# Two edits near the end of an attention stage: idle transposes confined to the last slot, and the last element's expert shares computed between its pick and its ranks

## What is computed

```
x = layernorm(x + attn(x, x, causal=True),  ln1)
x = layernorm(x + attn(x, ctx, causal=False), ln2)      # 16 heads of width 16
w = softmax(x @ router_w + router_b)                    # 8 experts
topw, topi = top_k(w, 2);  topw = softmax(topw)         # the two shares of a row
out = sum over e of combine[t, e] * (gelu(x @ w1[e] + b1[e]) @ w2[e] + b2[e])
x = layernorm(x + out, ln3)
```

## Time and profile before

| | us |
|---|---|
| median of 3 runs | 1198.77 |
| lowest, highest | 1197.58, 1203.42 |
| the profiled execution, its own time | 1199.14 |
| its span from first to last instruction | 1197.4 |
| attention block ends (barrier), on the span's clock | 880.5 |
| expert block | 880.5 to 1197.4 |

### The profile page before, as it was taken

One profiled execution on the slowest core, in us unless ns is written; L12 is line 12 of the kernel. 1 busy time (PEld: TensorE's weight loads), 2 busy tenths in 40 slices (PEclk: granted clock), 3 DMA queues, 4 the chain that ended last, 5 costly groups with the idle time before them and its releaser, 6 DMA issues. The chain is left out here.

```text
span 1197.4 us, 27891 instructions
## 1 busy us (share of the span) xinstructions
PE 1078.9 (90%) x9323; PEld 899.4 (75%) x9323; DVE 845.6 (71%) x2539; ACT 759.7 (63%) x1587; POOL 519.6 (43%) x736
## 2 busy tenths in 40 slices
PE   8688989999999999998899989888989999999960
PEld 7356666768888888876667666655779999999960
DVE  2777888777766666657777677664368888888856
ACT  4355565667666666655566666545258898888842
POOL 4355555322122213445667346442333454444554
PEclk9699999999999999999999999998989999999995
DMA  7685756654344433445656556531646877877774
GB/s 168 99 182 80 90 82 115 91 95 65 52 63 63 72 54 54 77 55 77 85 129 116 114 116 108 91 71 58 228 151 181 250 252 229 239 229 234 232 198 145
DMA packets 110893, 152.41 MB, mean 127 GB/s; under 512 B 23104, under 2 KB 95296, under 8 KB 104384
## 3 DMA queue, kind: packets, MB, share of 16 engines
q1 hardware_dynamic: 100560, 138.64, 52.2%
q0 software_dynamic: 8352, 10.80, 4.6%
q10 hardware_dynamic: 1872, 1.60, 1.1%
HBM read 78.39 MB, written 21.62 MB: 84 GB/s over the span
## 5 line engine op out<-in xcount | busy, mean ns | idle before, releaser
L996 ACT ACTIVATE probs<-s 128x384 f32<-128x384 f32 (+1 forms) x512 | 263.7, 541 | 127.2 <-PE s L771 113.8
L1080 DVE TENSOR_REDUCE neg_max<-s 128x2 f32<-128x512 f32 x256 | 168.1, 688 | 72.7 <-PE s L743 66.0
L771 PE MATMUL s<-q_stack,k_stack 98*128 98x256 bf16 (+1 forms) x1024 | 175.0, 261 | 10.6 <-ACT probs L996 8.1
L626 POOL TENSOR_SCALAR_AFFINE_SELECT probs<-probs 128x256 f32<-128x256 f32 x256 | 104.0, 418 | 173.4 <-ACT probs L996 171.0
L1077 DVE CUSTOM_DVE_ANT_0 s<-s,mask_qk 128x256 f32<-128x256 f32 x256 | 114.2, 446 | 64.4 <-PE s L740 56.6
L771 PEld LDWEIGHTS s<-q_stack,k_stack 98*128 98x128 bf16 x1024 | 87.2, 98 | 40.9 <-ACT probs L996 28.6
L793 PE MATMUL pv<-probs,v 128*32 128x256 f32 (+1 forms) x2048 | 111.1, 357 | 4.7 <-POOL probs L626 4.7
L743 PE MATMUL s<-k_stack,q_stack 96*128 96x256 bf16 x512 | 95.6, 275 | 14.4 <-DVE neg_max L1080 11.9
L1467 PE MATMUL moe<-rows_hi,e_w_hi 128*128 128x256 f32 x368 | 103.6, 282 | 2.0 <-DVE rows_lo L1585 2.0
L1467 PE MATMUL moe<-e_w_hi,e_hidden_hi 128*128 128x256 f32 x368 | 104.6, 284 | 0.0
L1467 PE MATMUL moe<-rows_hi,e_w_lo 128*128 128x256 f32 x368 | 103.0, 280 | 0.0
(11 more groups left out here) (209 smaller groups left out, 2913.1 us busy)
## 6 DMA issues: line engine op xcount, KB each, us to landing
w<-in_expert_w SPq DMA_DIRECT2D x26, 1024.0 KB, 5.4
k_stack<-k_part SPq DMA_DIRECT2D x192, 128.0 KB, 4.0
q_stack<-q_part SPq DMA_DIRECT2D x180, 128.0 KB
w_next<-in_expert_w SPq DMA_DIRECT2D x22, 1024.0 KB, 5.3
rows<-slots_x SPq DMA_DIRECT2D x25, 256.0 KB
slots_x<-filler SPq DMA_DIRECT2D x8, 518.0 KB
cT<-in_context SPq DMA_DIRECT2D x16, 256.0 KB, 5.7
e_b<-in_expert_b SPq DMA_DIRECT2D x24, 128.0 KB
```

Of the source, the lines that this page charges most:

```text
L626: pool.affine_select(out=blocks, in_=blocks, compare_op=ALU.is_ge, fill=0.0, base=0, pattern=[[0, TILES], [1, P]], channel_multiplier=-1). ...
L771: last = pe.matmul(dst[:, kt * S:kt * S + S - q0], k[:, kt * P:(kt + 1) * P], q[:, q0:S], start=True, stop=True)
L996: act.activation(probs_of(n, hd)[:, 0:width], s2[hd % 2][:, 0:width], ACT.Exp, scale=SCALE).then_inc(probs_ready, 1)
L1080: dve.tensor_reduce(neg_max[:, :, hd], src[:].rearrange("p (t s) -> p t s", t=TILES), AX_X, ALU.max, negate=True).then_inc(s1_free, 1)
```

## The change

The condition of the 12 transposes goes from n >= 27 to n == 31, and that of the 10 from lanes 2 to 6 to lane 6 alone. The `share` steps of lane 7 get times of their own, ahead of `rank` and `place`.

```diff
-DRAIN = NCALL - 5
+LAST_SHARES = (67.0, 68.0, 68.3, 70.0)
@@ plan_call
-        steps += [(at + later, "share", lane, i) for i, at in enumerate(AT["shares"])]
+        steps += [(at + later, "share", lane, i) for i, at in enumerate(LAST_SHARES if lane == B - 1 else AT["shares"])]
@@ scores
-                if n >= DRAIN and hd == H - 2:
+                if n == NCALL - 1 and hd == H - 2:
                     pe.wait_ge(u_ready, weighed_so_far[0])
                     idle(WARM_EXPS)
@@ final_T
-                if 2 <= lane < B - 1:
+                if lane == B - 2:
                     idle(WARM_NORM, dst)
```

## The result

The changed kernel took 1202.68 us (median of 20 runs, 1199.41 to 1207.4), the kernel before 1198.45 us (20 runs, 1195.96 to 1203.42). The ratio is 1.0033, 95% interval 1.0024 to 1.0041, so 2.9 to 4.9 us slower, centre 4.0. The forecast was 2 us faster (1196.8, range 1193.0 to 1202.0). The sign was wrong, and the median lies 0.7 us over the range; the change is still within the 0.5% in which I had put 0.91.

What follows compares the result with a forecast made beforehand. It took PE as busy 90% of the span, with unread transposes on the path in slots 27 and 28 only. Terms -3.5 + 0 + 2.4 - 0.9 = -2.0 took 1199.1 to 1197.1, with runs' median 0.4 lower: 1196.8, range 1193.0 to 1202.0.

Steps and rivals of the forecast that it cites:

- Slots 27 and 28: First parts of both slots shorten by 1.75 us each without the batches: -3.5 us, bounds 0 and -4.9.
- rival (D): Second parts of slots 27 and 28 shrink too: -4.9 + 2.4 - 0.9 = -3.4 us, 1195.4; chance 0.08.
- Rival (C): Second parts of slots 27 and 28 swallow their first parts' gain: +1.5 us, 1200.3; chance 0.15.
- Slots 29 and 30 start nothing earlier: PE waits for ACT and POOL behind the batches there, so removal gives 0 us at an unchanged clock.
- That they fall, and where: PE's clock falls once each in slots 29 and 30, near 794 to 799 and 821 to 826 us.
- Rival (A): The clock holds through slots 29 and 30: -3.5 - 0.9 = -4.4 us, 1194.4; chance 0.12.
- What a fall costs: Slower clock in slots 29 and 30: 1.2 us a slot, +2.4 us in all, bounds 0 and +6.8.
- the short spell: The 3.40 us stretch at 1.2 GHz near 851 in the earlier trace, taken as each fall's length in slots 29 and 30.
- Rival (B): Falls in slots 29 and 30 last 6.81 us and reach PE-bound work: +2.4 us in all, 1201.2; chance 0.22.
- The shares: Lane 7's last share comes 0.9 us earlier and all of it reaches the barrier: -0.9 us, bounds -0.9 and +0.3.
- The sum: Whole kernel: -3.5 + 0 + 2.4 - 0.9 = -2.0 us, forecast 1196.8; chance 0.43.

Runs made afterwards that it cites:

- `cut_27_28_shares`: Kernel before without the 12 and 10 unread transposes in slots 27 and 28 alone, plus lane 7's shares moved ahead: ratio 0.9974, repeated 0.9977.
- `cut_27_28_fill`: `cut_27_28_shares` plus 22 unread transposes in slot 29, 8 before head 7's maxima product and 14 before head 11's: 0.9942 of the kernel before, repeated 0.9959.

## Why the prediction was wrong

**Slots 27 and 28: right.** Forecast -3.5 us; the traces give 55.5 to 52.0, so -3.5, and timing gives -2.9 (-5.2 to -0.6). But that the two agree to the tenth is luck. The first parts shrank by 1.38 and 1.39 us, not 1.75, since POOL pauses 0.49 us ahead of the inverse root (L566) in slots 27 and 28 and not in slot 26, whether the batches are there or not. The rest is slot 28's second part (19.20 to 17.92 in the first pair), which the sum left alone and I had as bound and rival (D). It isn't bound to the edit either: slot 28 takes 28.3 to 28.4 us in four traces with the batches and 27.1 in three, among them both further traces of the kernel before. What the edit surely takes out is the 1.4 us a slot. Rival (C), the gain swallowed, is out.

**Slots 29 and 30 start nothing earlier: right.** POOL is waited for instead, 1.24 and 1.40 us, and the final transposes start 6.44 and 6.11 us behind L750 (6.36 and 6.06 before).

**That they fall, and where: right.** Forecast 794 to 799 and 821 to 826 us on the old clock; 794.4 and 825.1, that is 796.2 and 826.0 when counted from each slot's L750. Rival (A) is out.

**What a fall costs: this is the step that failed.** I took from the earlier trace rows "the short spell", 3.4 us, for each of the two slots, and 0.7 of half of it. Of the two factors one held. The price per microsecond at 1.2 GHz was about right: forecast 2.4 us for 6.8, 0.35 each; measured 6.6 us by timing (5.9 by the table) for 23.9 - 4.9 = 19.0 us more of it, 0.35 (0.31), and 0.26 by the plain medians. The length was wrong by a factor of near 3: the two spells last 6.8 to 10.2 us each in the four traces without either batch, and a shorter one follows at about 812 us, as it did before. Rival (B) named this mechanism and gave it 6.8 us a slot and +2.4 in all; it had the right side and was still short. The upper bound of the sum's term, +6.8, holds the measured 6.6 by luck: it put spells that were too short at a price, half of each microsecond, that was too high. The range's upper end, 1202.0, went by rival (B), and the 6.81 us behind it, the longest spell of the trace in these slots, was no bound: it was seen in a slot that kept its transposes. The Trainium skill's price, half the throttled time ("TensorE: Matmul & The Clock Gate", section "Terms"), would give an estimated 9.5 us for 19 us; the runs show 6.6 (4.0 to 9.3), probably because ACT and POOL are waited for through part of the spells.

Why the spells last so long is not settled. What the timelines show is that PE has waits for POOL and ACT and eight router products in them, and that the clock is back at 2.4 GHz only within or behind the value products of L793, in both slots of all four traces.

**The shares: right in the trace, not resolved by timing.** Forecast -0.9; in the traces 14.5 to 13.6, -0.9, though the two further traces of before have 13.9 with the old order; timed -0.6 (-2.5 to +1.4).

**The sum.** With the terms as the traces measured them, -3.5 + 5.9 - 0.9 = +1.5; as timed one by one, -2.9 + 6.6 - 0.6 = +3.1; the whole change, +4.0 (2.9 to 4.9). The timed terms agree with the whole within their intervals. The 2.5 us between the traces' sum and the whole stays open. More time at 1.2 GHz in the start or the expert block isn't the reason, since the clocks of all executions show none. But both stretches scatter by more than 2.5 us from trace to trace, and five traces of the two kernels can't tell whether one of them is longer in the changed kernel as a rule.

**The page of before.** I read the dips of the strip in the 28th and 30th slice as the end of the attention block. The 28th is the spell at 810; the 30th runs from 868 to 898 us, and its dip is a spell at 881.6 to 888.5, behind the barrier. Nothing in the sum hangs on it.

## What to carry to other kernels

Work that nobody reads has two prices, and both must be looked up at its place: remove it where it makes the work behind it late (here slots 27 and 28, full of other products), and leave it where the engine waits afterwards anyway (slots 29 and 30), because there it was free and the clock fell without it. When a forecast needs the length of a slow spell, don't take it from a stretch that was kept busy; ask what work could bring the clock back once the filler is gone (here the value products of L793, as far as the traces show), and let the bound reach to the end of that work. And where stretches with the same instructions differ by microseconds between two traces, time the parts of a change apart before reading a cause from one pair, and compare the clocks of all executions, not of one.

## What the hardware showed

- One program differs from trace to trace in the same three slots: the kernel before spent 10.2, 3.4 and 6.8 us at 1.2 GHz there, `cut_27_28_shares` 0 and 6.8; and the slots 27 and 28 of the kernel before took 56.1 us once and 54.8 twice.
- The eight router products (eight columns each) took 1.06 us at 2.4 GHz and 1.88 us at 1.2 GHz. All four traces without the two batches had them inside a spell; no run here tells whether they are a reason for it.
- The clock can come back while PE runs little but transposes that nobody reads: in `cut_27_28_fill` 75 of them run from 868.2 to 877.2 us with nothing else on PE, right behind twelve others, the router and the rank products, and the spell that began at 866.1 ends at 869.5.
- The expert block took 316.8 to 324.0 us in 16 traces of the same code, 319.0 to 324.0 on one chip, a scatter as large as any effect studied here. It is not at 2.4 GHz throughout: 41 to 50 us of it are at 1.2 GHz, most of them at its end.
